# Down-projection on int8 integers, normalised input kept in the buffer, and GpSimd in the gate-up stage

## The chip, the cores and the metric

The kernel runs on one core of a Trainium2 chip. The metric is device time in microseconds (us) of one launch. It uses five engines: TensorE (PE in the profile), VectorE (DVE), ScalarE (ACT), GpSimd (POOL) and the queue of SyncE (SP), which issues every transfer.

## The reference

One transformer layer over 32 images of 256 tokens, width 256, with a quantised gated feed-forward part behind it:

```
h = patches(x) @ W.T + b
h = h + attention(layernorm(h))
# feed-forward, on n = layernorm(h)
xs = sigmoid(clip_x) * max|n| / 127            # one scale for the whole tensor
xq = clip(round(n / xs), -128, 127)            # integers
gate, up = xq @ q(w_gate).T, xq @ q(w_up).T    # 256 -> 704, rows of the weights quantised
a  = silu(gate * scales) * up * scales
as_ = sigmoid(clip_down) * max|a| / 127        # again one scale for the whole tensor
aq = clip(round(a / as_), -128, 127)
out = h + (aq @ q(w_down).T) * scales          # 704 -> 256
```

The two maxima run over everything: no group of tokens can be quantised before every image is normalised, and none can enter the down-projection before every product is there. They cut the kernel into three stages.

## The kernel before, in words

Stage A, attention, takes image after image (IMAGES = 32) in a software pipeline: step `x` works at once on images x+3 to x-1, each engine in a written order (`step` in each engine's block, driven by `over_images`). At its end `residual` (L1261) writes the new h in place over the h from the embedding, in `h_all`; SyncE's `store_h1` sends it to `out`; `norm2_stats` to `normalise2` form the normalised rows in a tile of their own, `xn2`, for the maximum only (`peak_of`, L1313), and L1305 and L1306 keep mean and 1/deviation of all images. `h_all` is the tail of the large buffer `act_all`.

Between A and B, TensorE turns the quantised weights (L658 to L671) once the last image is through; VectorE reduces 32 maxima to one for each partition (L1374), GpSimd's `partition_all_reduce` (L1096) spreads the maximum over the partitions, and VectorE forms the scale.

Stage B, gate and up, takes 16 groups (NG) of 512 token columns (GT). The input is quantised anew from h: ScalarE scales 4 tiles of 256 columns (`scale_tile`, L930), VectorE rounds by adding and clips above (`round_x`, L1394), ScalarE clips below and makes bf16 (`clip_below`, L938), TensorE turns it (`turn_x`, L685), ScalarE copies it out of PSUM (`turned`, L945). Then for 6 tiles of rows (m = 0 to 5, the last with half the columns): gate product and up product on TensorE (L699, L705) in banks 2+m%3 and 5+m%3, silu on ScalarE (L954), and gate times up on VectorE (`product`, L1400) into `act_all`, all in f32. Twice a group VectorE takes the maximum of what was written (`act_peak_of`, L1410). A bank is free again when its silu or its product is done.

Between B and C the second maximum is spread in the same way (L1434, L1099, L1437, L1438).

Stage C, down, takes the same 16 groups. Each of the 6 tiles is rounded by a scale and an added constant (`round_act` on VectorE, L1445, or `scale_and_round` on ScalarE, L983), clipped on both sides on VectorE (`clip_act`, L1453), and lowered to bf16 integers on ScalarE (`lower`, L993). TensorE multiplies (L738); VectorE scales the result out of PSUM (`scale_down`, L1461) and adds h1 (`add_h`, L1470) in `h_in`, a ring of 4 buffers that SyncE loads from `out` (L378) and stores to `out` (L384). The load of group g+2 is issued behind the store of group g.

The order of each engine is the order of the code: there is no scheduler. Semaphores carry the rest.

## Time and profile before

| | us |
|---|---|
| median of 3 runs (1014.97 to 1017.15) | 1015.62 |
| profiled execution | 1015.05 |
| its span, first to last instruction | 1013.3 |
| TensorE busy | 831.9 (82%) |
| VectorE busy | 791.0 (78%) |
| ScalarE busy | 700.7 (69%) |
| GpSimd busy | 448.3 (44%) |

The busy shares are means over three stages. By the instructions, stage A lasts until 778.4 us (L1374 ends), the passage to stage B until 790.85 (the first L699), stage B until 916.8 (the last L1410 ends), and stage C from 918 to the end. GpSimd does nothing in B and C but one `partition_all_reduce`. The chain of work that ended last lies by 48% on TensorE, 23% on VectorE, 23% on issue and 4% on ScalarE.

Starts of successive instructions on one engine lie closer together than their durations, since one begins while the one ahead drains: for a stream of instructions the distance of starts counts (called the step here), for one that is waited for, its duration.

### The profile page before, as it was taken

To read this page: it belongs to the slowest core of one execution; us is meant where nothing else is said; L and a number is where in the kernel's file an instruction comes from. 1 tells how busy PE (TensorE), PEld (TensorE's weight loads), DVE (VectorE), ACT (ScalarE), POOL (GpSimd) and SP (SyncE) were. 2 spreads that over 40 slices of the span, in tenths; PEclk is the share of its full clock that TensorE was granted. 3 is DMA by queue.
4 is the path that set the end of the run, shared out by engine and by line. 5 is a ranking of instruction groups with operands and counts; after the bars stand their busy time and mean duration, and the time that the engine had idled before them with its cause. 6 is when DMAs were issued, how large, how long until landed. Compare 5 with 4: busy or idle time off the path is not lost.

```text
span 1013.3 us, 27043 instructions
## 1 busy us (share of the span) xinstructions
PE 831.9 (82%) x9057; PEld 486.1 (48%) x9066; DVE 791.0 (78%) x1564; ACT 700.7 (69%) x1147; POOL 448.3 (44%) x485
## 2 busy tenths in 40 slices
PE   3689999999999999999999999999874676774665
PEld 2355555555555555555555555555433333332332
DVE  5756777777777777777777777777774699998998
ACT  3266776666667776666677766666753899987996
POOL 1555566666555656666656566666531000000000
PEclk8789999999999999999999999999998899998998
DMA  7001111111111111111111111111000000003565
GB/s 252 27 2 38 39 37 36 36 36 36 57 52 36 36 36 36 36 36 49 60 36 36 36 36 36 36 47 38 12 12 22 0 1 0 0 0 125 166 195 178
DMA packets 33153, 50.34 MB, mean 50 GB/s; under 512 B 2016, under 2 KB 28384, under 8 KB 33120
## 3 DMA queue, kind: packets, MB, share of 16 engines
q1 hardware_dynamic: 33120, 49.91, 15.6%
q8 instruction: 19, 0.31, 0.1%
q14 instruction: 14, 0.11, 0.0%
HBM read 33.13 MB, written 16.78 MB: 49 GB/s over the span
## 4 chain that ended last, share of the span: by engine, by line
PE 48%; issue 23%; DVE 23%; ACT 4%; POOL 1%; DVEq 1%; DMA 0%; ACTq 0%; POOLq 0%
PE pair L433 10%; DVE act_all L1197 8%; PE pair L458 6%; PE pair L504 5%; PE pair L511 5%; PE pair L542 5%; PE pair L577 5%; DVE act_all L1238 3%; PE pair L488 3%; PE pair L526 3%; PE pair L546 2%; PE pair L566 2%; DVE act_all L1453 2%; ACT act_all L983 2%; DVE act_all L1246 1%
## 5 line engine op out<-in xcount | busy, mean ns | idle before, releaser
L1197 DVE TENSOR_REDUCE act_all<-pair 128x8 f32<-128x1024 f32 x192 | 235.2, 1225 | 101.4 <-PE pair L511 100.8
L833 ACT ACTIVATE act_all<-pair 128x768 f32<-128x768 f32 x256 | 207.9, 812 | 130.5 <-PE pair L528 130.2
L1018 POOL TENSOR_SCALAR_AFFINE_SELECT act_all<-act_all 128x512 f32<-128x512 f32 x256 | 163.4, 643 | 98.9 <-ACT act_all L833 98.7
L1061 POOL TENSOR_TENSOR act_all<-act_all 128x2 f32<-128x2 f32 x64 | 60.8, 951 | 210.8 <-DVE act_all L1230 139.0
L433 PE MATMUL pair<-act_all 128*128 128x256 f16 (+1 forms) x960 | 118.6, 278 | 9.3 <-DVE act_all L1133 9.3
L825 ACT ACTIVATE act_all<-pair 128x1024 f16<-128x1024 f16 x64 | 65.7, 1027 | 76.7 <-PE pair L488 76.7
L433 PEld LDWEIGHTS pair<-act_all 128*128 128x128 f16 (+1 forms) x960 | 91.6, 99 | 26.6 <-issue 15.3
L504 PE MATMUL pair<-act_all,eye_b 128*128 128x512 bf16 x256 | 78.5, 389 | 26.6 <-DVE act_all L1197 25.9
L542 PE MATMUL pair<-act_all 128*32 128x256 f32 x1024 | 81.8, 391 | 1.3 <-POOL act_all L1018 1.2
L1056 POOL TENSOR_TENSOR act_all<-act_all 128x1280 f16<-128x1280 f32 x31 | 81.0, 2611 | 1.3 <-ACT act_all L763 1.3
L511 PE MATMUL pair<-act_all 32*128 32x128 f16 x1536 | 76.7, 218 | 0.8 <-DVE act_all L1197 0.8
L458 PE MATMUL pair<-act_all 128*128 128x384 f16 x384 | 75.7, 335 | 1.5 <-DVE act_all L1268 1.5
L526 PE MATMUL pair<-act_all 64*128 64x256 f16 x512 | 72.6, 280 | 5.0 <-ACT act_all L833 2.6
L511 PEld LDWEIGHTS pair<-act_all 32*128 32x128 f16 x1536 | 43.5, 93 | 67.3 <-issue 66.0
L954 ACT ACTIVATE ffn<-pair,gate_scale 128x512 f32<-128x512 f32 x96 | 62.4, 650 | 11.2 <-DVE act_all L1400 6.6
L1400 DVE SCALAR_TENSOR_TENSOR act_all<-pair,gate_scale,ffn 128x512 f32 (+1 forms) x96 | 63.1, 699 | 8.3 <-ACT ffn L954 5.0
L699 PE MATMUL pair<-ffn,wg_t 128*128 128x512 bf16 x153 | 47.2, 387 | 24.1 <-ACT ffn L945 13.9
L1037 POOL TENSOR_TENSOR act_all<-act_all 128x320 f32<-128x320 f32 x64 | 53.9, 864 | 17.4 <-ACT act_all L779 17.4
L1099 POOL PARTITION_ALL_REDUCE small<-small x1 | 0.3, 350 | 134.4 <-DVEq L1435 134.4
L528 PE MATMUL pair<-act_all 64*128 64x128 f16 x512 | 56.3, 216 | 0.0
L699 PE MATMUL pair<-ffn,wu_t 128*128 128x512 bf16 x158 | 48.2, 387 | 9.5 <-DVE act_all L1400 9.5
L488 PE MATMUL pair<-act_all 128*128 128x128 f16 x640 | 52.9, 222 | 1.0 <-DVE act_all L1254 0.8
(141 smaller groups left out, 1758.8 us busy)
## 6 DMA issues: line engine op xcount, KB each, us to landing
act_all<-x_t SPq DMA_DIRECT2D x32, 640.0 KB, 4.0
out<-act_all SPq DMA_DIRECT2D x32, 256.0 KB, 2.2
ffn<-out SPq DMA_DIRECT2D x16, 512.0 KB, 4.6
out<-ffn SPq DMA_DIRECT2D x16, 512.0 KB, 3.2
act_all<-w_down SPq DMA_DIRECT2D x1, 704.0 KB, 8.8
act_all<-w_emb SPq DMA_DIRECT2D x1, 640.0 KB, 4.0
ffn<-w_gate SPq DMA_DIRECT2D x1, 640.0 KB, 7.5
ffn<-w_up SPq DMA_DIRECT2D x1, 640.0 KB, 8.0
```

Of the source, the lines that this page charges most:

```text
L433: mm = pe.matmul(b[:, 0:D], xs[0:k, sx, c, tb * P:(tb + 1) * P], we[0:k, sw, c, :], start=(c == 0 and (sx, sw) == PARTS[0]), stop=(c == KC ...
L458: mm = pe.matmul(b[:, 0:QKV_COLS], xn_t[:, sx, c, tb * P:(tb + 1) * P], wqkv[:, sw, c, :], start=(c == 0 and (sx, sw) == PARTS[0]), stop=( ...
L488: mm = pe.transpose(b[:, o:o + 64].bitcast(FP16), stack[:, tb, 2 * p:2 * p + 2, :].rearrange("p h k -> p (h k)"), eye_h)
L504: pe.matmul(max_bank[j], eye_b[:, :], tri_b.rearrange("p (a t) -> p a t", a=1).to_broadcast([P, GROUPS, P]), start=True, stop=False, skip_ ...
L511: mm = pe.matmul(max_bank[j][:, g * P:(g + 1) * P], max_op[rows, g, qt * P:(qt + 1) * P], max_op[rows, 4, kt * P:(kt + 1) * P], start=(qt ...
L526: pe.matmul(b[:, 0:TOKENS], k[rows, kp, 0:P], q[rows, i, :], start=True, stop=True)
L542: pe.matmul(b[32 * kv:32 * kv + 32, cols:cols + TOKENS], v[:, 0, kv, :], probs[:, 4 * (g % 2) + kv, 0:2, :], start=True, stop=False, skip_ ...
L699: mm = pe.matmul(b[:, :], w[:, c, m * P:(m + 1) * P], xs[:, c, :], start=(c == 0), stop=(c == DC - 1))
L833: act.activation(probs[:, o:o + 2, 0:3, :].rearrange("p h k s -> p h (k s)"), pair[1][:, :].rearrange("p (h c) -> p h c", h=2)[:, :, 0:3 * P],
L1018: pool.affine_select(out=p, in_=p, pattern=[[0, 4], [1, P]], compare_op=ALU.is_ge, fill=0.0, base=0, channel_multiplier=-1).then_inc(maske ...
L1056: pool.tensor_tensor(x_parts[v.parity][:, 1], xt[v.parity], x_parts[v.parity][:, 0], ALU.subtract).then_inc(x_low_ready, 1)
L1197: dve.tensor_reduce(to.rearrange("p (g k) -> p k g", g=GROUPS)[:, first:first + 2, :], pair[2][:, :].rearrange("p (k g t) -> p k g t", k=2 ...
```

## The change

1. Stage A: `residual` writes h1 into one of two small tiles `h1[k]`, from which it is stored and normalised; the normalised rows go into `h_all`, in the place of h. The tile `xn2` and the two copies of mean and deviation go away. `residual` gains a wait for the store of two images before, and a semaphore increment of its own.
2. The weights are turned in three parts inside TensorE's step of the last image; the silu table is loaded ahead of the weight copies.
3. Both maxima are spread by a TensorE product with an identity (`spread_peak`) and a VectorE maximum over its 128 columns.
4. The input becomes an int8 tile `x8` (one multiplication with conversion), then bf16: for group 0 on VectorE and ScalarE, for all others on GpSimd (`quantise_x`, `widen_x`), two groups ahead.
5. Of the six products of a group GpSimd makes m = 1 and m = 4 (`multiply`), from a copy of the up product that ScalarE takes out of PSUM (`copy_up`). VectorE keeps 0, 2, 3 and 5, and takes the maximum of a group's second half behind product 0 of the next group.
6. Stage C: VectorE quantises a group in two instructions from f32 to int8 (`quantise`), two groups ahead; ScalarE widens to bf16 in two (`widen`); `scale_down` and `add_h` take all 1024 columns at once.
7. The loop of stage A starts two images later and runs 12 times in place of 13.

```diff
+POOL_M = (1, 4)
+DVE_M = (0, 2, 3, 5)
-FIRST_LOOPED, LOOPED_PAIRS = 2, (IMAGES - 6) // 2
+FIRST_LOOPED, LOOPED_PAIRS = 4, (IMAGES - 8) // 2
...
+            def spread_peak(col):
+                pe.matmul(bank[1][:, 0:P], small[:, col:col + 1].to_broadcast([P, P]), eye_k[:, :],
+                          start=True, stop=True, skip_group_check=True).then_inc(peak_spread, 1)
...
+            def copy_up(g, m):
+                j = POOL_M.index(m)
+                act.wait_ge(up_done, g * IM + (m + 1))
+                wait(act, act_by_pool, g * len(POOL_M) + (j - 1))
+                act.activation(up_sb[j], bank[5 + m % 3][:, :], ACT.Copy, scale=gate_scale[:, IM + m:IM + m + 1]
+                               ).then_inc(up_copied, 1)
...
+                    if m in POOL_M:
+                        wait(act, act_by_pool, g * len(POOL_M) + POOL_M.index(m))
+                    else:
+                        wait(act, act_ready, g * len(DVE_M) + (DVE_M.index(m) - 1))
...
+            def widen(g, k):
+                for half, (lo, hi) in enumerate(A_HALVES):
...
+                    act.activation(aq[k][:, lo:hi], q8[k][:, lo:hi], ACT.Copy).then_inc(aq_ready, 1)
...
+            def quantise_x(g):
...
+                pool.tensor_scalar(x8[k], h_all[:, g * GTT * D:(g + 1) * GTT * D], small[:, 7:8], 0.0,
+                                   ALU.mult, ALU.add).then_inc(x_quantised, 1)
+            def widen_x(g):
...
+                pool.tensor_scalar(xq[k].rearrange("p t e -> p (t e)"), x8[k], 1.0, 0.0, ALU.mult, ALU.add
+                                   ).then_inc(xq_ready, 1)
+            def multiply(g, m):
+                j = POOL_M.index(m)
+                pool.wait_ge(up_copied, g * len(POOL_M) + (j + 1))
+                pool.wait_ge(silu_ready, g * IM + (m + 1))
+                o = g * A_COLS + m * GT
+                pool.tensor_tensor(act_all[:, o:o + GT], up_sb[j], silu[m % 3], ALU.mult).then_inc(act_by_pool, 1)
...
             def residual(x):
                 w = x + -1
+                wait(dve, h1_stored[w.parity], w.half * 16)
                 dve.wait_ge(done["out"], w.n + 1)
-                dve.scalar_tensor_tensor(h_of(w), shared[JOBS.index(("out", 0)) % 2][:, :], 1.0 / W_UNIT, h_of(w),
+                fence(dve)
+                dve.scalar_tensor_tensor(h1[w.parity].rearrange("p b e -> p (b e)"),
+                                         shared[JOBS.index(("out", 0)) % 2][:, :], 1.0 / W_UNIT, h_of(w),
...
-                dve.tensor_copy(mean2[:, bass.ds(w.n * TB, TB)], mv2[:, :, 0])
-                dve.tensor_copy(rstd2[:, bass.ds(w.n * TB, TB)], rstd2s)
...
+            def quantise(g, k, half):
+                lo, hi = A_HALVES[half]
+                if half == 0 and (not isinstance(g, int) or g >= 2):
+                    dve.wait_ge(aq_ready, g * 2 - 2)
+                dve.tensor_scalar(q8[k][:, lo:hi], act_all[:, bass.ds(g * A_COLS + lo, hi - lo)], small[:, 13:14],
+                                  QMAX, ALU.mult, ALU.min).then_inc(a_quantised, 1)
```

How the order of instructions moves, at three places.

ScalarE, stage B, one whole group (ffn is the area of silu tiles, `x_buf`, `xq` and `xq_t`; pair is PSUM). Before:

```order
L954 ACTIVATE ffn<-pair,gate_scale 128x512
L930 ACTIVATE ffn<-act_all,mean,rstd 128x256
L954 ACTIVATE ffn<-pair,gate_scale 128x512
L938 ACTIVATE ffn<-ffn,small 128x1024
L954 ACTIVATE ffn<-pair,gate_scale 128x512
L930 ACTIVATE ffn<-act_all,mean,rstd 128x256
L954 ACTIVATE ffn<-pair,gate_scale 128x512
L930 ACTIVATE ffn<-act_all,mean,rstd 128x256 x2
L954 ACTIVATE ffn<-pair,gate_scale 128x512
L945 ACTIVATE ffn<-pair 128x1024
L954 ACTIVATE ffn<-pair,gate_scale 128x256
```

After (L986 is silu, L966 `copy_up`, L974 `turned`):

```order
L986 ACTIVATE ffn<-pair,gate_scale 128x512 x2
L966 ACTIVATE ffn<-pair,gate_scale 128x512
L986 ACTIVATE ffn<-pair,gate_scale 128x512 x2
L974 ACTIVATE ffn<-pair 128x1024
L986 ACTIVATE ffn<-pair,gate_scale 128x512
L966 ACTIVATE ffn<-pair,gate_scale 128x512
L986 ACTIVATE ffn<-pair,gate_scale 128x256
```

The four scalings L930 and the clip L938 have gone; two copies of the up product have come, each behind the silu of its own m, and `turned` stands behind m = 3 in place of m = 4.

GpSimd, behind the last masks of stage A. Before (L1096 and L1099 are the two `partition_all_reduce`):

```order
L1018 AFFINE_SELECT act_all<-act_all 128x4x128 x8
L1061 TENSOR_TENSOR act_all<-act_all 128x2 x2
L1096 ISA
L1096 ISA small<-small 128x1
L1099 ISA small<-small 128x1
```

After (L1114 `quantise_x`, L1122 `widen_x`, L1130 `multiply`; the rows from the third L1114 on repeat until group 13):

```order
L1030 AFFINE_SELECT act_all<-act_all 128x4x128 x8
L1073 TENSOR_TENSOR act_all<-act_all 128x2 x2
L1114 TENSOR_SCALAR ffn<-act_all,small 128x1024
L1122 TENSOR_SCALAR ffn<-ffn 128x1024
L1114 TENSOR_SCALAR ffn<-act_all,small 128x1024
L1130 TENSOR_TENSOR act_all<-ffn 128x512
L1122 TENSOR_SCALAR ffn<-ffn 128x1024
L1130 TENSOR_TENSOR act_all<-ffn 128x512
L1114 TENSOR_SCALAR ffn<-act_all,small 128x1024
```

Both reduces have left; each group has two conversions and two products in turn.

VectorE, stage C, one group. Before (L1445 `round_act`, L1453 `clip_act`, L1461 `scale_down`, L1470 `add_h`):

```order
L1445 TENSOR_SCALAR act_all<-act_all,small 128x512 x2
L1445 TENSOR_SCALAR act_all<-act_all,small 128x256
L1453 TENSOR_SCALAR act_all<-act_all 128x512 x4
L1461 TENSOR_TENSOR ffn<-pair,down_row 128x512
L1453 TENSOR_SCALAR act_all<-act_all 128x512
L1470 TENSOR_TENSOR ffn<-ffn 128x512
L1461 TENSOR_TENSOR ffn<-pair,down_row 128x512
L1453 TENSOR_SCALAR act_all<-act_all 128x256
L1470 TENSOR_TENSOR ffn<-ffn 128x512
```

After (L1495 `scale_down`, L1487 `quantise` of group g+2, L1504 `add_h`):

```order
L1495 TENSOR_TENSOR ffn<-pair,down_row 128x1024
L1487 TENSOR_SCALAR wu_t<-act_all,small 128x1536
L1504 TENSOR_TENSOR ffn<-ffn 128x1024
L1487 TENSOR_SCALAR wu_t<-act_all,small 128x1280
```

Thirteen instructions have become four, on more columns each, and the quantising stands behind `scale_down` and looks two groups ahead in place of one.

## Rows read from the trace of the kernel before

**Rows 1.** Busy time by stage: stretch, its length, busy us of each engine, clock, DMA
```profile
778.40:790.80 12.40, 1.03 (x8) 0.90 (x10) 3.73 (x10) 9.21 (x15) 0.38 (x1) 0.59 0.00 0
790.80:916.80 126.00, 89.84 (x559) 41.60 (x566) 117.98 (x143) 111.28 (x182) 0.00 (x0) 0.99 0.01 1
916.80:918.00 1.20, 0.00 (x0) 0.00 (x0) 0.58 (x4) 0.00 (x0) 0.35 (x1) 0.70 0.68 224
918.00:1013.30 95.30, 56.95 (x384) 29.66 (x384) 87.72 (x209) 82.10 (x144) 0.00 (x0) 0.89 0.56 173
```

**Rows 2.** Timeline, VectorE, one group of the gate-up stage: start, us, line, tiles
```profile
838.75 0.68 DVE L1394 TENSOR_SCALAR ffn<-ffn 128x1024 f32<-128x1024 f32 x1
839.35 1.48 DVE L1410 TENSOR_REDUCE peak<-act_all  x1
840.74 2.06 DVE L1400 SCALAR_TENSOR_TENSOR act_all<-pair,gate_scale,ffn 128x512 f32 x3
846.49 0.68 DVE L1394 TENSOR_SCALAR ffn<-ffn 128x1024 f32<-128x1024 f32 x1
```

**Rows 3.** Timeline, ScalarE, the same group
```profile
843.78 0.68 ACT L954 ACTIVATE ffn<-pair,gate_scale 128x512 f32<-128x512 f32 x1
844.35 1.02 ACT L945 ACTIVATE ffn<-pair 128x1024 bf16<-128x1024 bf16 x1
845.25 0.48 ACT L954 ACTIVATE ffn<-pair,gate_scale 128x256 f32<-128x256 f32 x1
```

**Rows 4.** Groups by form, GpSimd, attention stage: count, busy, mean ns, idle before
```profile
L1018 POOL TENSOR_SCALAR_AFFINE_SELECT act_all<-act_all 128x512 f32<-128x512 f32 x256 | 163.4, 643 | 98.9 <-ACT act_all L833 98.7
L1051 POOL TENSOR_TENSOR act_all<-act_all 128x640 f32<-128x640 f32 x32 | 49.6, 1549 | 0.3 <-POOL act_all L1026 0.2
```

**Rows 5.** One line's instructions, L1160: min/median/max ns, first and last start
```profile
L1160 DVE TENSOR_SCALAR ffn<-ffn x2: 960/960/960, 26.8 to 33.9; 128x1536 bf16<-128x1536 f32 x2
```

**Rows 6.** Timeline, from the end of the attention stage to the first gate-up
```profile
770.83 2.72 PE L577 MATMUL pair<-act_all 128*128 128x256 f16 x12 [1.50 <-DVE act_all L1275]
...
778.19 0.19 DVE L1374 TENSOR_REDUCE small<-peak 128x1 f32<-128x32 f32 x1
782.37 0.38 POOL L1096 PARTITION_ALL_REDUCE small<-small  x1 [5.82 <-issue]
782.78 0.21 DVE L1377 TENSOR_SCALAR small<-small 128x1 f32<-128x1 f32 x1 [4.41 <-POOL small L1096]
789.33 1.00 ACT L945 ACTIVATE ffn<-pair 128x1024 bf16<-128x1024 bf16 x1
790.85 0.63 PE L699 MATMUL pair<-ffn,wg_t 128*128 128x512 bf16 x1 [1.81 <-ACT ffn L945]
```

**Rows 7.** Timeline, TensorE, the same product one image earlier
```profile
760.85 1.47 PE L577 MATMUL pair<-act_all 128*128 128x256 f16 x12 [0.45 <-DVE act_all L1275]
```

**Rows 8.** Timeline, VectorE, one group of the down-projection and the last add
```profile
952.13 1.43 DVE L1453 TENSOR_SCALAR act_all<-act_all  x4
953.47 0.69 DVE L1461 TENSOR_TENSOR ffn<-pair,down_row 128x512 f32<-128x512 f32 x1
957.66 1.43 DVE L1453 TENSOR_SCALAR act_all<-act_all  x4
...
1009.19 0.69 DVE L1470 TENSOR_TENSOR ffn<-ffn 128x512 f32<-128x512 f32 x1
```

**Rows 9.** Timeline, TensorE, down-projection at the start and later
```profile
922.57 1.80 PE L738 MATMUL pair<-wd_t,wu_t 128*128 128x256 bf16 x8
...
959.04 1.13 PE L738 MATMUL pair<-wd_t,wg_t 128*128 128x256 bf16 x8 [0.64 <-ACT wg_t L993]
```

**Rows 10.** Groups by form, ScalarE, down-projection stage
```profile
L993 ACT ACTIVATE wg_t<-act_all 128x512 bf16 x28 | 16.1, 621 | 5.2 <-DVE act_all L1453 5.2
```

**Rows 11.** DMA issues, KB each, median us to landing
```profile
ffn<-out SPq DMA_DIRECT2D x16, 512.0 KB, 4.6
```

**Rows 12.** Busy time, 918 to 923, while the first four groups load
```profile
918.00:923.00 5.00, 2.09 (x11) 1.32 (x12) 4.93 (x15) 4.98 (x9) 0.00 (x0) 0.50 1.06 347
```

More of the change, by code:

```diff
@@ L21 @@
 FP16 = mybir.dt.float16
+INT8 = mybir.dt.int8
 ALU = mybir.AluOpType
@@ L1472, in pass_c @@
             def pass_c(turn, slot, ahead=True):
-                g = 4 * turn + slot
+                g, k = 4 * turn + slot, slot % 2
+                scale_down(g, k)
                 if ahead:
-                    for m in BY_VECTOR:
-                        round_act(g + 1, m)
-                    for m in range(4):
-                        clip_act(g + 1, m)
+                    quantise(g + 2, k, 0)
                 dve.wait_ge(g_loaded[slot], turn * 16 + 16)
-                for t2 in range(2):
-                    scale_down(g, slot, t2)
-                    if ahead:
-                        clip_act(g + 1, 4 + t2)
-                    add_h(g, slot, t2)
@@ L1486, in _ @@
-            for m in range(IM + 1):
-                if m in BY_VECTOR:
-                    round_act(0, m)
-                if m >= 1:
-                    clip_act(0, m - 1)
+                add_h(g, slot)
+                if ahead:
+                    quantise(g + 2, k, 1)
+            for g in range(2):
+                quantise(g, g, 0)
+                quantise(g, g, 1)
             link(dve.tensor_scalar(down_row[:, :], down_row[:, :], small[:, 12:13], None, ALU.mult))
@@ L1497, in _ @@
             for slot in range(4):
-                pass_c(NG // 4 - 1, slot, ahead=(slot < 3))
+                pass_c(NG // 4 - 1, slot, ahead=(slot < 2))
 def kernel(**inputs):
```

355 lines of the change are left out of this document (176 added, 179 removed).

## The prediction

> **What bounds the kernel now.** I read the page first (slices and chain), then the windows by stage, then the timelines of one group in each stage, then the waits. Stage A is a chain through TensorE and VectorE that the change hardly touches; it has 778.4 of the 1013.3 us. Behind it lie a passage of 12.4 us in which TensorE is busy for 1.0, stage B of 126.0 us and stage C of 95.3 us [rows 1]. So at most 234.9 us are in play.
>
> Stage B: a group takes 7.74 us (two starts of L1394, 838.75 and 846.49) [rows 2]. VectorE is busy for 118.0 of 126.0 us, ScalarE for 111.3, TensorE for 89.8 [rows 1]: VectorE bounds it, with ScalarE close behind. Stage C: a group takes 5.53 us (952.13 to 957.66) [rows 8], VectorE busy for 87.7 of 95.3 us, ScalarE 82.1, TensorE 57.0 [rows 1]: VectorE again. The passage is a row of waits, the longest being 4.41 us for the maximum to be spread: GpSimd's own 0.38 us are preceded by 5.82 us of issue [rows 6], some setting up that happens once.
>
> **Stage A.** VectorE loses two copies for each image and gains a wait and an increment in front of `residual`. The copies stand ahead of a wait for ScalarE, so taking them out gains nothing in the loop. The increment may lie on the chain; bounds are -1 and +2 us over 32 images, and I take 0. The wait for the store is for one issued two steps (some 45 us) earlier, and hidden. Behind the last image, the 12 matmuls of `out_project` took 2.72 us at half clock [rows 6], where the image before took 1.47 [rows 7]; TensorE had idled ahead of them. The weight transposes now stand in those idles, so the clock (1.2 GHz there, 2.4 GHz one image earlier) should stay up: -1.0, bounds 0 and -1.2. The maximum over images then is ready at 778.38 - 1.0 = 777.4.
>
> **Passage A to B.** From the end of L1374 to the first gate matmul it took 790.85 - 778.38 = 12.5 us. Now: wait and one f32 matmul at half clock 0.7, VectorE maximum 0.3, scale and reciprocal 0.45 (L1377 has 0.21), int8 conversion of 1024 columns 0.7 as L1394's 0.68 [rows 2], ScalarE widening 1.2, eight transposes at half clock 1.2, `turned` 1.0 [rows 6], four handovers of 0.1 to 0.2 among these: 6.3. Two scalings and the clip on ScalarE have left, and the 4.4 us have become about 1.0. The weight copies and the table load run earlier, under the wait for `out_project` and the norm. Start of stage B: 783.7, against 790.85. Bounds for this term, 5.5 to 8.
>
> **Stage B.** Steps from the timelines: silu 0.57 (843.78 to 844.35), `turned` 0.90 (844.35 to 845.25) [rows 3], product 0.66 (a third of 2.06 less the drain), maxima 1.39 (839.35 to 840.74) and some 1.66 [rows 2]. For each group:
> - VectorE: 3 x 0.66 + 0.40 + 1.66 + 1.39 = 5.4 us (7.37 before, 118.0 over 16).
> - ScalarE: 5 silus 2.85, one half 0.38, two `copy_up` 1.14, `turned` 0.90: 5.3 us.
> - TensorE: what it did before, 89.8 us for 16 groups [rows 1], 5.6 us.
> - GpSimd: two products of 512 columns, two conversions of 1024. A product: L1051 takes 1.55 us for 640 columns [rows 4], so 1.24 by proportion, with a fixed part 1.28. The conversions are the unknown. From below, L1018 (one input) takes 0.64 for 512 [rows 4], so 1.28; from above, the two-input rate of L1051 gives 2.48. A conversion has one input, so I take 1.5. Sum 2 x 1.28 + 2 x 1.5 = 5.6; with the bounds 5.1 and 7.5.
>
> None of these alone sets the time: a ring does. GpSimd reads silu slot 1 for m = 4, and the next group's silu of m = 1 writes it. Round the ring: `multiply` 1.28, silu m = 1 0.57, `copy_up` 0.57, silus 2 and 3 1.14, `turned` 0.90, silu 4 0.57, `copy_up` to its end 0.66, two handovers 0.12 each: 5.93 us. GpSimd's 5.6 fit within. I take 5.94 for each group, a gain of 1.80. Outside 15 periods stage B had 125.9 - 15 x 7.74 = 9.8 us; a group with fewer products ends about 1.0 earlier, and the half clock at the start, till now hidden below VectorE, costs 1.5. So 15 x 5.94 + 8.8 + 1.5 = 99.4, against 125.9. The bounds of the conversions make it 99 to 122.
>
> The rule against this part is in the Trainium skill, GPSIMD Engine Reference, section "Elementwise — side-by-side cycle accounting": a two-input operation costs GpSimd 2.6 cycles for each element where VectorE needs one. Our row agrees with it (1.55 us for 640 columns are 2.4 ns for each, where L1410 takes 1.48 for 1280). The same section has 1.8 cycles at 1.2 GHz as its best loop otherwise: 1.54 us for 1024 columns, an estimate by that page; no row shows it, and the sum would be the same by it, since GpSimd then still ends within the ring.
>
> **Passage B to C.** It took 1.2 us, in which GpSimd was busy for 0.35 [rows 1]: the second spreading was cheap, some 0.5 us with its handovers. Now it is a matmul and a maximum, 1.0: 1.7 us in all, slightly longer.
>
> **Stage C.** VectorE for each group: L1160 makes 1536 f32 columns into bf16 in 0.96 us [rows 5], which is two columns a cycle against L1410's one. If int8 is written as bf16 is, `quantise` takes steps of 0.87 and 0.74. `scale_down`, 512 columns in 0.69 [rows 8] with a step of 0.60, becomes 1.13 for 1024, and `add_h` likewise. Sum 0.87 + 0.74 + 1.13 + 1.13 = 3.88 us, against 5.53. ScalarE: L993 has 0.62 for 512 [rows 10]; by the slope of `turned` and silu, 1536 and 1280 take 1.38 and 1.17: 2.6 us, hidden. TensorE: 8 matmuls 1.13 at full clock [rows 9], so 24 in some 2.9, hidden; at half clock 1.80 for 8, 5.2 for 24, which is not hidden. Stage C had 0.89 of the clock on the mean [rows 1] at a lower load than it gets now. DMA: 1.05 MB in 3.88 us are 270 GB/s; the four first loads ran at 347 GB/s [rows 12]. A load lands 4.6 us after its issue [rows 11], and has 2 x 3.88 less 1.6 = 6.1. It fits, by little.
>
> The lead-in is longer: both halves of group 0 are quantised first (1.8), widened 1.5, and 24 matmuls, the first 16 at half clock, take 4.5: first `scale_down` at +8.2. Then 14 x 3.88 = 54.3, two groups without quantising 5.6 (the last waits for its widening), and the store 1013.3 - 1009.88 = 3.4 behind the last add [rows 8]. Sum 71.5, against 95.3.
>
> **Sum.** 777.4 + 6.3 + 99.4 + 1.7 + 71.5 = 956.3 us of span. The profiled execution took 1015.05 for a span of 1013.3, 1.75 more: 958.1. Its time lies 0.6 below the median of the runs, 1015.62: 958.7, say **959 us**, 5.6% less.
>
> **Rivals.**
> 1. GpSimd becomes the bound of stage B. At 2.48 us for a conversion its work is 7.5 us for each group, and VectorE's gain is given back: 14 groups by 1.5 us are 22, so 981 us. For it: the two-input rate in the trace, a narrowing to one byte that no row shows. Against: L1018 at half that rate. A conversion at 2.0 gives 6.6, 9 us more and 968.
> 2. VectorE writes int8 at one column a cycle. `quantise` is then 1.67 + 1.41 in place of 1.61, a group of stage C 5.35, and 16 x 1.47 = 23 us are lost: 982. For it: no row of before writes a byte. Against: L1160 mixes two widths and keeps the double rate.
> 3. DMA or TensorE's clock sets stage C. If loads and stores hold a group at 4.5 us (233 GB/s), 0.6 x 15 = 9 us more: 968.
> 4. Slower than before. GpSimd's conversion by way of int8 costs over 3.5 us, 1.4 times its two-input rate. To cancel 57 us, a group of stage B must take 5.94 + 57/14 = 10.0, thus conversions of 3.7 us; at 4.2 it would be 1030. Nothing in the rows goes that high.
> 5. The change doesn't do what it says: `multiply` and the products don't overlap, because ScalarE waits for GpSimd at each of the two. Then each group pays 1.5 us for each of two waits in place of one: 7.4 us, 980.
>
> **Chances.** Forecast (953 to 965) 0.50; rival 1 in full or in part 0.17; rival 2 0.12; rival 3 0.09; rival 5 0.04; rival 4 0.03; better than 953, by stage A or the passages, 0.05. Range 948 to 984: the lower end has 5.5 us for the passage, the gain in stage A and a ring without the clock's 1.5; the upper end holds each of rivals 1, 2, 3 and 5 alone, not two together. A measurement of this kernel tells 0.2%, 2 us, from no change: faster 0.96, same 0.01, slower 0.03.
>
> **What would show it.** Right: groups of 5.9 to 6.0 us in stage B with silu m = 1 waiting for `multiply` and GpSimd conversions near 1.5 us; two `quantise` of 0.96 and 0.82; groups of 3.9 us in stage C with VectorE over 95% busy; TensorE's `spread_peak` done within 1 us; the first gate matmul near 784. Wrong: GpSimd never idle in stage B; a `quantise` of 1.75 us; VectorE waiting for the load or for down matmuls at half clock; stage A ending later than before.

## The result, and the profile after

The changed kernel took 962.05 us, the median of 4 runs (960.71 to 966.27), against 1016.38 us (1014.97 to 1019.67) for the kernel before on the same chip: a ratio of 0.947, 95% interval 0.944 to 0.950, so 54 us or 5.3% less. The forecast was 959 us, with 948 to 984 as its range.

The profiled execution took 966.27 us, span 964.5 us, and is the slowest of the four; the spans of the others were 961.3, 959.0 and 959.4 us. Why it is slow belongs to the reading below. Busy times by stage in it, in the same columns as [rows 1]:

```profile
784.70:791.20 6.50, 2.15 (x11) 1.56 (x13) 3.67 (x8) 2.08 (x2) 3.76 (x3) 0.50 0.00 0
791.20:889.10 97.90, 89.44 (x559) 39.52 (x565) 90.50 (x96) 86.35 (x143) 69.22 (x59) 0.99 0.00 1
889.10:891.00 1.90, 0.77 (x2) 0.50 (x2) 0.82 (x4) 0.00 (x0) 0.00 (x0) 0.50 0.76 254
891.00:964.50 73.50, 47.48 (x384) 31.73 (x384) 64.62 (x66) 43.72 (x32) 0.00 (x0) 0.92 0.73 221
```

Each row gives the stretch and its length, the busy us of TensorE, its weight loads, VectorE, ScalarE and GpSimd with their instruction counts, TensorE's granted clock, and DMA. Stage B fell from 126.0 to 97.9 us and stage C from 95.3 to 73.5 [rows 1]. In stage B TensorE is busy for the same 89 us, now 91% of the stage; VectorE fell from 118.0 to 90.5 us and ScalarE from 111.3 to 86.4, while GpSimd rose from nothing to 69.2. In stage C VectorE has 66 instructions in place of 209.

The passage between A and B, as the timeline has it (the rows that answer to [rows 6]):

```profile
784.51 0.19 DVE L1418 TENSOR_REDUCE small<-peak 128x1 f32<-128x32 f32 x1
784.75 0.80 PE L694 MATMUL pair<-eye_k,small 128*128 128x128 f32 x2 [3.55 <-DVE small L1418]
785.59 0.29 DVE L1420 TENSOR_REDUCE small<-pair 128x1 f32<-128x128 f32 x1 [0.89 <-PE pair L694]
...
786.37 0.75 DVE L1425 TENSOR_SCALAR ffn<-act_all,small 128x1024 int8<-128x1024 f32 x1
787.15 1.06 ACT L959 ACTIVATE ffn<-ffn 128x1024 bf16<-128x1024 int8 x1 [5.63 <-DVE ffn L1425]
788.26 1.03 PE L711 MATMUL pair<-eye_b,ffn 128*128 128x128 bf16 x8 [2.71 <-ACT ffn L959]
789.34 1.02 ACT L974 ACTIVATE ffn<-pair 128x1024 bf16<-128x1024 bf16 x1 [1.13 <-PE pair L711]
790.88 0.63 PE L729 MATMUL pair<-ffn,wg_t 128*128 128x512 bf16 x1 [1.58 <-ACT ffn L974]
```

Every link of the forecast's chain is there, one row each: from the end of L1418 at 784.70 to the first gate matmul it is 6.18 us, where 12.5 us stood before.

One group of stage B on ScalarE (first fence) and GpSimd (second), answering to [rows 3]:

```profile
834.79 0.69 ACT L986 ACTIVATE ffn<-pair,gate_scale 128x512 f32<-128x512 f32 x1 [0.45 <-POOL act_all L1130]
835.38 0.68 ACT L966 ACTIVATE ffn<-pair,gate_scale 128x512 f32<-128x512 f32 x1
835.95 1.26 ACT L986 ACTIVATE ffn<-pair,gate_scale 128x512 f32<-128x512 f32 x2
837.09 1.04 ACT L974 ACTIVATE ffn<-pair 128x1024 bf16<-128x1024 bf16 x1
...
840.67 0.69 ACT L986 ACTIVATE ffn<-pair,gate_scale 128x512 f32<-128x512 f32 x1 [0.45 <-POOL act_all L1130]
```

```profile
836.14 1.27 POOL L1130 TENSOR_TENSOR act_all<-ffn 128x512 f32<-128x512 f32 x1 [0.28 <-ACT ffn L966]
837.38 1.05 POOL L1122 TENSOR_SCALAR ffn<-ffn 128x1024 bf16<-128x1024 int8 x1
839.36 1.27 POOL L1130 TENSOR_TENSOR act_all<-ffn 128x512 f32<-128x512 f32 x1 [0.94 <-ACT ffn L966]
840.61 1.12 POOL L1114 TENSOR_SCALAR ffn<-act_all,small 128x1024 int8<-128x1024 f32 x1
```

The period is 840.67 - 834.79 = 5.88 us. Once a group ScalarE stands still for 0.45 us, and the row shows for whom: silu of m = 1 waits for GpSimd's product of m = 4, which ended at 840.63. GpSimd itself waits before both of its products; its conversions took 1.05 and 1.12 us.

One group of stage C on VectorE, answering to [rows 8], and its widening on ScalarE:

```profile
923.36 1.22 DVE L1495 TENSOR_TENSOR ffn<-pair,down_row 128x1024 f32<-128x1024 f32 x1
924.49 1.01 DVE L1487 TENSOR_SCALAR wg_t<-act_all,small 128x1536 int8 x1
925.42 1.22 DVE L1504 TENSOR_TENSOR ffn<-ffn 128x1024 f32<-128x1024 f32 x1
926.55 0.88 DVE L1487 TENSOR_SCALAR wg_t<-act_all,small 128x1280 int8 x1
927.35 1.22 DVE L1495 TENSOR_TENSOR ffn<-pair,down_row 128x1024 f32<-128x1024 f32 x1
```

```profile
925.62 1.48 ACT L1014 ACTIVATE act_all<-wg_t 128x1536 bf16<-128x1536 int8 x1 [0.87 <-DVE wg_t L1487]
927.47 1.27 ACT L1014 ACTIVATE act_all<-wg_t 128x1280 bf16<-128x1280 int8 x1 [0.37 <-DVE wg_t L1487]
```

VectorE has no gap: 1.13 + 0.93 + 1.13 + 0.80 = 3.99 us. ScalarE waits before each widening.

### The profile page after: what moved, and what is told of

It reads as the page before. It is cut to its first block, busy times and chain, and to the rows that moved or that the text cites. A ratio compares the mean times of both kernels' runs of the same rounds, so it can differ in the third digit from the quotient of the medians.

```text
span 964.5 us, 26048 instructions
## 1 busy us (share of the span) xinstructions
PE 831.7 (86%) x9061; PEld 490.0 (51%) x9070; DVE 735.9 (76%) x1309; ACT 632.9 (66%) x988; POOL 519.8 (54%) x545
## 4 chain that ended last, share of the span: by engine, by line
PE 55%; DVE 26%; issue 10%; ACT 4%; POOL 1%; DVEq 1%; DMA 1%; ACTq 0%; SPq 0%; POOLq 0%
PE pair L439 10%; DVE act_all L1240 9%; PE pair L464 7%; PE pair L510 6%; PE pair L517 5%; PE pair L548 5%; PE pair L583 5%; PE pair L729 4%; DVE act_all L1281 4%; PE pair L494 3%; PE pair L532 3%; PE pair L552 2%; ACT ffn L986 2%; PE pair L572 2%; DVE ffn L1504 2%
## 5 line engine op out<-in xcount | busy, mean ns | idle before, releaser
L439 PE MATMUL pair<-act_all 128*128 128x256 f16 (+1 forms) x960 | 120.7, 281 | 9.3 <-DVE act_all L1175 9.3
L986 ACT ACTIVATE ffn<-pair,gate_scale 128x512 f32<-128x512 f32 x96 | 60.2, 671 | 9.4 <-POOL act_all L1130 7.1
L774 PE MATMUL pair<-wd_t,act_all 128*128 128x256 bf16 (+1 forms) x384 | 47.5, 282 | 20.4 <-ACT act_all L1014 20.4
L1130 POOL TENSOR_TENSOR act_all<-ffn 128x512 f32<-128x512 f32 x32 | 40.7, 1273 | 27.7 <-ACT ffn L966 27.7
L563 PE MATMUL pair<-act_all 128*128 128x128 f32 x256 | 42.1, 288 | 14.6 <-DVE act_all L1231 13.8
L532 PEld LDWEIGHTS pair<-act_all 64*128 64x128 f16 x512 | 24.6, 93 | 55.5 <-issue 39.1
```

The lines of the kernel that those rows point to most:

```text
L439: mm = pe.matmul(b[:, 0:D], xs[0:k, sx, c, tb * P:(tb + 1) * P], we[0:k, sw, c, :], start=(c == 0 and (sx, sw) == PARTS[0]), stop=(c == KC ...
L532: pe.matmul(b[:, 0:TOKENS], k[rows, kp, 0:P], q[rows, i, :], start=True, stop=True)
L986: act.activation(silu[m % 3][:, 0:cols], bank[2 + m % 3][:, 0:cols], ACT.Silu, scale=gate_scale[:, m:m + 1]).then_inc(silu_ready, 1)
```

## The experiments

Line numbers shift by some lines from kernel to kernel; the names stay.

**e1_again: the changed kernel once more.** No edit.

> The changed kernel once more, unchanged. The theory of the start: its first profile lost some 5 us before image 1, where TensorE ran at half clock for longer than in the profile of before; nothing of the change lies there. So in another execution the residual of image 1 starts near 117 us or near 122 us as the clock happens to fall, and the time of the run goes along: 961 us median, single runs 960 to 966. Rival: code that the change lengthened costs 5 us at the start in every execution; then all profiles have image 1 at 121 to 122 us.

961.09 us median (960.34 to 963.19, 4 runs); ratio 0.946 (0.943 to 0.949). The span of the profiled execution was 959.4 us, 5.1 less than that of the first. The difference can be laid on one stretch. The first kernel's fence is the changed kernel in its first profile, the second is this run; both show VectorE's residual of image 1 and the busy times of 60 to 80 us:

```profile
121.86 0.69 DVE L1306 SCALAR_TENSOR_TENSOR act_all<-pair,act_all 128x512 f32<-128x512 f32 x1 [0.30 <-PE pair L583]
...
60.00:80.00 20.00, 16.87 (x158) 8.14 (x159) 11.71 (x18) 11.53 (x19) 13.08 (x14) 0.74 0.00 1
```

```profile
116.81 0.69 DVE L1306 SCALAR_TENSOR_TENSOR act_all<-pair,act_all 128x512 f32<-128x512 f32 x1 [0.30 <-PE pair L583]
...
60.00:80.00 20.00, 17.70 (x212) 10.45 (x214) 10.97 (x15) 12.45 (x21) 11.64 (x13) 0.91 0.01 1
```

In the first, TensorE had 0.74 of its clock in this stretch and got through 158 matmuls; here 0.91 and 212. That is 5.05 us at image 1, and it stays until the end. The kernel before stands at 0.91 too. The edit is empty, so this time is no fixed cost of the change; the runs of the kernel before spread as widely on this chip (1014.42 to 1020.24 us). I take this run where stage A is compared.

**e2_pool_1_3: another pair of products on GpSimd.**

```diff
-POOL_M = (1, 4)
-DVE_M = (0, 2, 3, 5)
+POOL_M = (1, 3)
+DVE_M = (0, 2, 4, 5)
+def occupant(g, m, by_pool, by_dve):
...
-                    if m in POOL_M:
-                        wait(act, act_by_pool, g * len(POOL_M) + POOL_M.index(m))
-                    else:
-                        wait(act, act_ready, g * len(DVE_M) + (DVE_M.index(m) - 1))
+                    wait(act, *occupant(g, m, act_by_pool, act_ready))
...
+                multiply(g, POOL_M[1])
...
-                multiply(g, POOL_M[1])
```

In words: GpSimd's order in a group becomes both products, then `widen_x` and `quantise_x`; on VectorE product 3 leaves and product 4 comes, and the first maximum of a group stands behind product 2 in place of product 3; `occupant` names the product whose end frees a slot or a bank.

> GpSimd multiplies m = 1 and m = 3 in place of 1 and 4, its widening stands behind both products, and VectorE takes its first maximum behind product 2. The ring (the next group's silu of m = 1 waits for the product of m = 4 in the same silu slot) is then longer by the silus of 4, 5 and 0. Theory ring: the group falls from 5.88 us to 5.7 to 5.76, where TensorE waits only for the turned input; stage B is 2 to 3 us shorter, 959 against 961. Rival, GpSimd's own work: it is the same 4.7 us, and the group stays at 5.88. Rival, TensorE is already the bound: no change either. In the trace ScalarE's waits for GpSimd (6.4 us over 14 groups) must go in the first case.

958.32 us (957.82 to 959.13, 4 runs); ratio 0.943 (0.940 to 0.946), and its highest run lies below the lowest of e1_again on the same chip. A group takes 840.09 - 834.28 = 5.81 us, and what ends ScalarE's idle time is TensorE:

```profile
834.28 0.69 ACT L990 ACTIVATE ffn<-pair,gate_scale 128x512 f32<-128x512 f32 x1 [0.16 <-PE pair L736]
...
840.09 0.69 ACT L990 ACTIVATE ffn<-pair,gate_scale 128x512 f32<-128x512 f32 x1 [0.17 <-PE pair L736]
```

ScalarE's wait for GpSimd has gone, with GpSimd doing the same amount of work: what set the 5.88 us was the ring, not the sum of GpSimd's work. But the next limit lies close below: the group got 0.07 us shorter, not the 0.12 to 0.18 expected, and TensorE, for which ScalarE now waits, has itself waited 0.50 us for a product of VectorE just before. That VectorE's maximum moved as well was not tested apart.

Not all of the gain is the ring's. The second maximum starts at 882.49 in place of 883.96, 1.5 us earlier. Another 0.9 us of the 2.4 between the two spans lies in stage C, which this edit doesn't touch: its first 48 matmuls took 6.76 us here and 7.43 in e1_again, since the half clock at their start lasted for less time.

**e3_turn_early: the turning one step earlier.** On top of e2, on TensorE and on ScalarE:

```diff
-                    if m == 3 and ahead:
+                    if m == 2 and ahead:
```

> As the one before, and the input of the next group is turned behind m = 2 in place of m = 3, on TensorE and on ScalarE. Theory: with the ring gone, TensorE's wait for the turned input (0.42 us in a group) is what is left, and one tile more of cover takes it away: 5.55 to 5.6 us for a group, TensorE never idle in stage B, 4 to 5 us less than the changed kernel: 957. Rival: ScalarE, with 5.3 us of work, then waits for gate products at other places, and the group stays at 5.7: 959.

963.16 us (961.20 to 966.64, 4 runs): slower than e2 by 4.8, a miss. A group takes 6.04 us and the wait for GpSimd is back:

```profile
834.27 1.27 ACT L990 ACTIVATE ffn<-pair,gate_scale 128x512 f32<-128x512 f32 x2 [0.45 <-POOL act_all L1134]
...
840.31 1.27 ACT L990 ACTIVATE ffn<-pair,gate_scale 128x512 f32<-128x512 f32 x2 [0.44 <-POOL act_all L1134]
```

The wait is now that of silu m = 0 (the first of the two in the row) for the product of m = 3. Silu of m = 3 and of m = 0 share slot 0, so with GpSimd at m = 1 and 3 there are two rings. Moving `turned` (0.9 us) ahead of m = 3 put it between `multiply` of m = 1 and the next user of its slot, but took it from the distance that `multiply` of m = 3 has until m = 0. An instruction on ScalarE lengthens one ring and pads another: it is the place that counts, with no work added. In the profiled executions stage B, from the first maximum to the second, took 106.1 us against 102.9 in e2, so 3.2 of the 4.8 us are seen there; this profile is of the fastest of the four runs.

**e4_add_on_gpsimd: VectorE's add moved to GpSimd.** In stage C `add_h` goes to GpSimd, with two tiles for the scaled product.

```diff
-                dve.tensor_tensor(y, y, scaled, ALU.add).then_inc(y_ready, 1)
+                pool.tensor_tensor(y, y, scaled[g % 2], ALU.add).then_inc(y_ready, 1)
...
-                if not isinstance(g, int) or g >= 1:
-                    dve.wait_ge(y_ready, g)
+                if not isinstance(g, int) or g >= 2:
+                    dve.wait_ge(y_ready, g - 1)
```

> Stage C: the add of h1 goes from VectorE to GpSimd, idle there, with two tiles for the scaled result. VectorE keeps 1.13 + 0.92 + 0.79 = 2.85 us for a group in place of 3.99. Theory A, no contention: GpSimd needs 2.14 ns for a column, 2.3 us for 1024, so the group is bound by the transfers (1.05 MB at the 347 GB/s seen, 3.0 us) or their latency, 3.1 to 3.4 us: 9 to 12 us less. Theory B, contention: two quantising instructions on VectorE (1.7 us for a group, two columns a cycle) and GpSimd's reads exclude each other, so GpSimd needs 2.3 + 1.7 = 4.0 us for a group or more: 3.9 to 4.4 us, no gain or up to 6 us lost, and GpSimd's adds show 3.2 to 4.0 us each. For B: a GpSimd mask beside the conversion L1160 took longer than its 0.64 us in the profile of before. By the Trainium skill, SBUF — State Buffer, section on who interferes with whom, B holds: the shared ports are an exclusive lock.

975.93 us in one run, 15 us slower than the change. This is one run, so its time stands with its trace only. VectorE in one group, then GpSimd:

```profile
929.14 1.21 DVE L1502 TENSOR_TENSOR act_all<-pair,down_row 128x1024 f32<-128x1024 f32 x1
930.27 3.90 DVE L1494 TENSOR_SCALAR wu_t<-act_all,small 128x1536 int8 x2
934.09 1.21 DVE L1502 TENSOR_TENSOR ffn<-pair,down_row 128x1024 f32<-128x1024 f32 x1
```

```profile
930.50 2.99 POOL L1150 TENSOR_TENSOR ffn<-ffn,act_all 128x1024 f32<-128x1024 f32 x1 [1.96 <-DVE act_all L1502]
```

VectorE lost an instruction of 1.13 us and its group grew from 3.99 to 4.95 us, because the two quantisations, 1.81 us together without company, take 3.90. The second of them ends at 934.17, 0.68 us behind GpSimd's add, and it takes 0.88 us alone: it ran once the add was nearly over. The add in turn took 2.99 us, against 2.34 for the last one of the kernel (968.42), which has no quantisation beside it. So the two engines took turns: beside an instruction of GpSimd that reads two tiles from SBUF, VectorE's quantisation stood still. The Trainium skill says the same (SBUF — State Buffer, section "SBUF: two separate sides"): the port pair that VectorE and GpSimd share is an exclusive lock for the length of an instruction, not a split of bandwidth; the trace agrees, with 3.90 for 1.81 us.

Of the two theories on record B holds, but it put the group at 3.9 to 4.4 us: the loss was larger, because the three stand in a row, `scale_down` 1.2 us, the add 3.0 and what is left of the quantisation 0.7. In stage B, where GpSimd was busy for 69 of 98 us, VectorE's instructions did not grow: the two maxima of a group took 1.48 and 1.74 us in both kernels, and a product 0.75 us with a product of GpSimd beside it or (e5) without.

**e5_products_on_vector: no product on GpSimd.** GpSimd keeps the two conversions, and `copy_up` falls away.

```diff
-POOL_M = (1, 4)
-DVE_M = (0, 2, 3, 5)
+POOL_M = ()
+DVE_M = (0, 1, 2, 3, 4, 5)
```

> All six products of a group on VectorE again, no copies of the up product; the conversions stay on GpSimd. VectorE's work is 5 x 0.66 + 0.40 + 1.66 + 1.39 = 6.75 us and a little idling. Theory (VectorE bounds as soon as the two products are back): 6.8 to 6.9 us for a group, stage B 14 to 16 us longer, 975 us. That would split the 1.86 us won for each group into 0.9 for the rounding and clipping taken off VectorE and ScalarE, and 0.95 for the two products. Rival: the ring with GpSimd was the cost of the offload and the offload gains little, under 6.4 us for a group, below 969.

972.52 us in one run. A group of stage B takes 6.73 us, as the distance of one maximum to the next shows:

```profile
820.88 1.48 DVE L1450 TENSOR_REDUCE peak<-act_all  x1
...
827.61 1.48 DVE L1450 TENSOR_REDUCE peak<-act_all  x1
```

The expectation, 6.8 to 6.9 us, had it slightly too long. So of the 1.86 us that a group lost, 1.01 came from taking the rounding off VectorE and ScalarE, and 0.85 from the two products.

**e6_all_reduce: the first maximum spread by GpSimd again.** `spread_peak` for the first maximum is replaced by the reduce:

```diff
-            pe.wait_ge(scales, 1)
-            spread_peak(4)
+            pool.wait_ge(scales, 1)
+            pool.partition_all_reduce(small[:, 5:6], small[:, 4:5], P, bass.bass_isa.ReduceOp.max).then_inc(
+                peak_spread, 1)
```

> The first maximum is spread by GpSimd's partition_all_reduce again, the second stays with TensorE. In the kernel before, GpSimd idled 5.82 us ahead of it with nothing in the trace to wait for, counted from its last instruction of stage A. Theory (a one-time setting up of 5.8 us, which starts once GpSimd is free): last GpSimd instruction of stage A, plus 5.8, plus 0.4, against a maximum spread 0.9 us after VectorE's reduce: the first gate matmul comes 3.3 to 3.7 us later, 965 us. Rival: the idle time was a handover that the shorter queue shortens, and the cost is under 1 us. If GpSimd has to set up again for its elementwise work behind, its first conversion starts later than 0.2 us after VectorE's signal.

964.42 us in one run, span 962.7 against 959.4 of e1_again: +3.3. From the start of VectorE's reduce to the first gate matmul it took 9.08 us in place of 6.06: +3.0, a little under the 3.3 to 3.7 expected. The rest are stage B (+1.2), stage C (-0.2) and an earlier end of stage A (-0.7). GpSimd and the wait on VectorE, and GpSimd's next instruction:

```profile
782.90 0.38 POOL L1131 PARTITION_ALL_REDUCE small<-small  x1 [5.72 <-issue]
783.31 0.21 DVE L1421 TENSOR_SCALAR small<-small 128x1 f32<-128x1 f32 x1 [4.31 <-POOL small L1131]
...
790.43 1.11 POOL L1112 TENSOR_SCALAR ffn<-act_all,small 128x1024 int8<-128x1024 f32 x1 [7.16 <-issue]
```

GpSimd's last work ahead of it ended at 777.18, the maximum was ready at 779.00, and the reduce ran only at 782.90: 5.72 us of setting up, of which 1.8 were hidden. Before it was 5.82 [rows 6].

The last row answers the question that the expectation left open: GpSimd's first conversion starts 7.16 us behind the reduce, although its scale was ready at 783.72. GpSimd had done elementwise work all through stage A, so this wait is not one of a first use. The idle time comes at each of the two changes of kind, from elementwise work to the reduce and back. In the kernel before, where nothing stood between the two reduces, the second took 0.35 us with no such time. That fits a set-up at each change; no run here has a second change to the reduce, so a cost of its first use is not excluded as well. The late conversion is felt in stage B: in its first group a silu waits 0.64 us for GpSimd, which in e1_again none does.

**e7_turn_at_end: the weights turned behind stage A.** The three parts stand behind the last image again:

```diff
-                if x.known and x.n == IMAGES:
-                    turn_weights(0)
...
+            for part_ in range(3):
+                turn_weights(part_)
```

> The three parts of the weight transposes stand behind stage A again, as in the kernel before. Theory (the transposes fill TensorE's idle time and hold its clock): out_project of the last image takes 2.7 us in place of 1.47, and the last residual comes 1.2 us later after the one of image 30. The weight copies on ScalarE then end about 3 us later, still ahead of the first widening, so nothing more: +1.2 us. Rival: the weight turning lies on the path to the first gate matmul, +3 us or more.

963.07 us in one run, span 961.4: +2.0 against e1_again. TensorE in this kernel, then in the changed one:

```profile
772.84 2.72 PE L583 MATMUL pair<-act_all 128*128 128x256 f16 x12 [1.50 <-DVE act_all L1317]
```

```profile
778.30 1.47 PE L583 MATMUL pair<-act_all 128*128 128x256 f16 x12 [0.57 <-DVE act_all L1321]
```

The last `out_project` is back at half clock, 2.72 us as in [rows 6]. From image 30's residual to the last one it takes 11.41 us, 9.72 with the transposes in the gaps, 11.22 before. This execution had image 1 at 116.07, 0.7 us earlier than e1_again, so behind image 1 it is 2.7 us longer: 1.7 in the last image, and most of the rest in stage B (99.6 us against 98.4), where the half clock lasted 4.8 us from the first gate matmul in place of 2.7. The 1.7 us are shown: TensorE's granted clock was 0.51 from 770 to 776 us here, and 1.00 from 770 to 778 in e1_again. The part in stage B is not, since e9, whose kernel is the changed one up to stage C, has 99.9 us there.

**e8_constant_scale: quantising by a constant.** This kernel multiplies by 0.5 in place of the scale, so its output isn't the layer's.

```diff
-                dve.tensor_scalar(q8[k][:, lo:hi], act_all[:, bass.ds(g * A_COLS + lo, hi - lo)], small[:, 13:14],
+                dve.tensor_scalar(q8[k][:, lo:hi], act_all[:, bass.ds(g * A_COLS + lo, hi - lo)], 0.5,
```

> Stage C: quantise multiplies by the constant 0.5 in place of the scale held in SBUF (the output is wrong by that scale). A group took 3.99 us where 3.88 was forecast; quantise lasts 1.015 and 0.885 us where L1160 takes 0.96 for 1536 columns with constants. Theory A: the 0.055 us go to reading the scale; then quantise takes 0.96 and 0.83, and the group 3.88. Theory B: they go to writing one byte in place of two; then 1.015 and 0.885 stay. For A: L1445 with the scale from SBUF took 0.48 us and L1453 with constants 0.43, both 512 columns of f32.

```profile
936.45 1.21 DVE L1495 TENSOR_TENSOR ffn<-pair,down_row 128x1024 f32<-128x1024 f32 x1
937.59 0.95 DVE L1487 TENSOR_SCALAR wu_t<-act_all 128x1536 int8 x1
...
939.59 0.82 DVE L1487 TENSOR_SCALAR wu_t<-act_all 128x1280 int8 x1
940.32 1.21 DVE L1495 TENSOR_TENSOR ffn<-pair,down_row 128x1024 f32<-128x1024 f32 x1
```

The quantisations take 0.95 and 0.82 us in place of 1.01 and 0.88, and a group 3.87 in place of 3.99. Stage C from the second maximum (883.52) to the end is 73.7 us against 75.4 in e1_again: 14 groups by 0.12 us. One run, 958.9 us. So theory A holds: the time goes to reading the scale, not to writing one byte.

**e9_split_quantise: ScalarE takes a share of the quantising.**

```diff
+Q_HALVES = ((0, 3 * GT), (3 * GT, 4 * GT))
...
+                lo, hi = Q_HALVES[1][1], A_COLS
...
+                act.activation(q8[k][:, lo:hi], act_all[:, bass.ds(g * A_COLS + lo, hi - lo)], ACT.Copy,
+                               scale=small[:, 13:14]).then_inc(a_by_scalar, 1)
...
-                lo, hi = A_HALVES[half]
+                lo, hi = Q_HALVES[half]
```

> The changed kernel, but in stage C ScalarE rounds the last 768 of a group's 2816 columns to int8 itself, so VectorE writes 1536 + 512 instead of 1536 + 1280. Theory: stage C is VectorE's sum, 1.14 + 0.925 + 1.14 + 0.79 = 3.99 us a group in the changed kernel; with the second rounding cut to about 0.40 us (0.79 - 0.055 of fixed reading, scaled by 512/1280, and 0.1 of start) the sum is 3.60 us, and ScalarE, at 1.35 + 1.15 for the widening and about 0.8 for 768 columns, stays below with 3.3 us. Over 14 groups -5.5 us: about 956 us against 961 to 962. Rival: DMA or the landing of a load takes over at 3.8 us or more (the queues moved 260 GB/s in stage C and would have to move 290), then 958 to 960 us and VectorE's add waits for the load. A second rival: ScalarE, which now reads the same act_all while VectorE does, becomes the bound at 3.8 to 4.0 us and nothing is gained.

955.03 us (953.88 to 955.74, 4 runs); ratio 0.938 (0.934 to 0.941).

```profile
932.71 1.21 DVE L1505 TENSOR_TENSOR ffn<-pair,down_row 128x1024 f32<-128x1024 f32 x1
933.84 1.01 DVE L1497 TENSOR_SCALAR wu_t<-act_all,small 128x1536 int8 x1
933.99 0.92 ACT L1012 ACTIVATE wu_t<-act_all,small 128x768 int8 x1
...
934.88 2.80 ACT L1023 ACTIVATE act_all<-wu_t 128x1536 bf16<-128x1536 int8 x2
935.90 0.48 DVE L1497 TENSOR_SCALAR wu_t<-act_all,small 128x512 int8 x1
936.30 1.21 DVE L1505 TENSOR_TENSOR ffn<-pair,down_row 128x1024 f32<-128x1024 f32 x1
...
910.00:940.00 30.00, 21.89 (x197) 15.66 (x196) 30.00 (x35) 29.64 (x25) 0.00 (x0) 1.00 0.96 289
```

A group takes 3.59 us (3.60 expected). From the second maximum to the end it is 69.3 us, 6.1 less than in e1_again. Of these, 14 groups by 0.40 us are 5.6; the half clock at the start of the stage was shorter too (6.64 us for the first 48 matmuls, 7.43 in e1_again). The last row is the steady stretch from 910 to 940 us: VectorE is busy without a gap, ScalarE, estimated at 3.3 us a group, for 29.64 of 30 us, and the DMA engines for 0.96 of the time at 289 GB/s (262 GB/s and 0.86 in e1_again). DMA held VectorE up for 1.2 us in all, at the last two adds, so it doesn't bound yet; but all three stand close to their limit, and a further cut on VectorE alone would find the other two.

**e10_both: e2 and e9 together.**

> The two gains together: GpSimd takes products 1 and 3 instead of 1 and 4, with the widening behind both (5.82 us a group in stage B instead of 5.88, and the last maximum earlier; 958.3 us alone), and ScalarE rounds the last 768 columns of a group in stage C (-5.5 us by the sum, if the theory of the other run holds). They act in different stages, so they should add up: about 953 us. If DMA bounds stage C, 955 to 957 us.

954.89 us (953.88 to 959.44, 4 runs); ratio 0.939 (0.935 to 0.943). The expected 953 was not reached, and it can't be told from e9. Group times are those of the parts (3.59 us in stage C), and the second maximum is 1.9 us earlier than in e9 (882.14 against 884.02); but the first `scale_down` comes 9.9 us behind the maximum, and 9.2 in e9. The 0.7 us between them is TensorE's half clock again: the first 48 matmuls of stage C took 7.37 us here and 6.64 in e9, on the same code. Of the 1.9 us, 1.1 is left in the spans (952.2 against 953.3).

**e11_no_fence: the increment ahead of the residual left out.**

```diff
                 dve.wait_ge(done["out"], w.n + 1)
-                fence(dve)
```

> The changed kernel without the semaphore step that it puts on VectorE ahead of the residual of each image in stage A. Theory: that step is why every second image takes 22.69 us a pair instead of 22.60, 0.95 us over stage A's loop; without it the first maximum falls at about 778.5 us instead of 779.5 and the run ends about 1 us earlier (960). Rival: the pair's period is set by TensorE's clock or by GpSimd, and the step costs nothing: 961 to 962 us with pairs of 22.69 us.

966.25 us in its one run, which by itself looks like a loss. The trace says otherwise. TensorE had 0.74 of its clock from 60 to 80 us, as in the first profile of the change, and the residual of image 1 stands at 122.00. From there to image 29 (images counted from 0; the expectation of e12 calls it image 28) it takes 628.95 us against 630.21 in e1_again (747.02 - 116.81), since each second image takes 22.59 us in place of 22.69. All ten other profiles with the increment have 629.9 to 630.2 us there, whatever their clock at 60 to 80 us. So the cost of the increment is shown, 1.3 us, and the total of this run says nothing about it.

**e12_both_no_fence: e10 without the increment.**

> The kernel with both gains (products 1 and 3 on GpSimd, ScalarE rounding the last 768 columns), and without the semaphore step on VectorE ahead of the residual. Theory: the step costs 0.1 us in every second image of stage A, so image 28 comes 1.0 to 1.15 us earlier behind image 1, as in the kernel without it alone; nothing behind stage A depends on it, so about 953.8 us against 954.9. Rival: the clock at the end of stage A, which differs from run to run by 1.4 to 2 us at image 30, hides it, and the median stays at 954 to 956 us.

952.72 us (951.50 to 954.95, 4 runs); ratio 0.9375 (0.936 to 0.939). This is the lowest median of all, 9.3 us below the change, and its interval lies below that of the change. Image 1 to image 29 took 628.91 us. Against e10 the intervals overlap, so the 1.3 us of the increment are shown in the loop and not in the total. e9, e10 and e12 all beat the changed kernel; among the three the times don't decide.

## Why the prediction was right

| term, us | forecast | first profile | e1_again |
|---|---|---|---|
| first maximum (end) | 777.4 | 784.70 | 779.67 |
| to the first gate matmul | 6.3 | 6.18 | 5.87 |
| to the second maximum (start) | 99.4 | 98.22 | 98.42 |
| to the first quantise | 1.7 | 1.98 | 1.97 |
| to the end | 71.5 | 73.42 | 73.47 |
| span | 956.3 | 964.5 | 959.4 |

In e1_again the five terms are off by +2.3, -0.4, -1.0, +0.3 and +2.0 us, 3.1 in all: the mechanisms behind stage A came as forecast, and each stage within 2 us. In the first profile the first term is off by 7.3 us, 5 of them the clock at 60 to 80 us, for which the forecast had no term. So the median's 3 us are in part luck: errors of both signs partly cancel, and it depends on which clock the four executions met. One sign on record for being wrong came true, stage A ending later than before; it does in both profiles. The misses are in three terms:

- **Stage A**, forecast 1.0 us early, is 1.3 late in e1_again (first maximum at 779.48, before 778.19 [rows 6]). Three pieces add up. The loop from image 1 to 29 takes 630.21 in place of 628.84: +1.37, of which e11 and e12 take 1.26 to 1.30 back by leaving the increment out. The forecast had set this at 0 within bounds of -1 and +2. The last image, with the transposes in TensorE's gaps, gained more than was said, 9.72 against 11.22: -1.50, where the forecast had -1.0 and -1.2 as its bound. And image 30 took 18.14 in place of 16.77: +1.37, as the granted clock shows, first in e1_again, then in e9:

```profile
759.00:765.00 6.00, 5.38 (x42) 2.97 (x44) 1.63 (x4) 2.91 (x5) 1.91 (x3) 0.57 0.01 3
```

```profile
759.00:765.00 6.00, 4.17 (x58) 2.58 (x56) 2.58 (x7) 3.38 (x5) 1.78 (x3) 1.00 0.01 3
```

  That piece comes and goes: with 1.00 the image takes 16.8 us in e4, e5, e8, e9 and e10, which all have the changed kernel's stage A. The last section shows that stage B then gives it back.
- **Stage B** is right by its mechanism. The ring was put at 5.93 us and measured 5.88; the wait of silu m = 1 for GpSimd is there, e2 takes it away and e3 brings one back in the other slot. The conversions, taken at 1.5 us within 1.28 and 2.48, took 1.05 and 1.12, below the lower bound, and it changed nothing, since GpSimd had room in the ring. Rival 1 needed 2.0 and more, rival 4 3.7, and rival 5 a wait at both products, where there is one.
- **Stage C** is 1.9 us longer than forecast. A quantisation with its scale in SBUF costs 0.06 us more than with a constant (e8), 0.12 a group, 1.7 in all: e8's 3.87 us is the forecast's 3.88. The estimate had been drawn from L1160, 0.96 us for 1536 columns [rows 5], which has a constant. The rest lies at the end, where the last add waits 0.49 us for its load, and in the lead-in: the first `scale_down` came at +8.3 us for the 8.2 forecast, though the three parts given for it add up to 7.8. Rival 2 is out: int8 keeps the double rate. Rival 3 is out as a bound at 3.99 us a group, and e9 went to 3.59. TensorE ran at 0.92 of its clock and stayed hidden.

The passage was right at 6.3, and e6 shows what the spreading is worth in it: 3.0 us. The prediction read GpSimd's 5.82 us of issue as a set-up that happens once; e6 has a second one of 7.16 us, on the way back to elementwise work, so that reading does not stand, though no term of the sum hangs on it. The Trainium skill's 1.8 cycles for an element (GPSIMD Engine Reference, "Elementwise — side-by-side cycle accounting"), 1.54 us for 1024 columns by that page as an estimate, is too high here: measured 1.12 with conversion to int8 and 1.05 back. The same section has a bound by the ports of about 1.03 cycles for bodies of at most two operations, an estimate of 0.88 us before any fixed cost, and the trace lies nearer to that.

What stays open: why TensorE is granted its clock earlier in some executions than in others. No experiment set it off or kept it away. The stretches go together, though: the five profiles with the full clock at image 30 (e4, e5, e8, e9, e10) are just those with 1.00 between 60 and 80 us; the other eight of the changed kernels have 0.74 to 0.91 there. The kernel before has 0.91 there and the full clock at image 30, so it isn't a rule.

## What to carry to other kernels

When work moves to an idle engine, don't compare sums of work only: follow each buffer that two engines share around its ring, with its waits. Here it gave the group to 1%, with GpSimd's conversions put at 1.5 us each where they took 1.1. An instruction between two users of a slot belongs to the ring's price; e3 lost 0.23 us a group by moving one that was needed elsewhere as padding. And a stage whose one engine has no gap is shortened by handing over pieces of an instruction to a neighbour with gaps, as e9 did with ScalarE; e4 did it with GpSimd and lost, because its add and VectorE's quantisation took turns.
